# Gelu stage of a fused conv, expert and mixer block: bank rotation and fold of the partition groups

## The chip, the cores and the metric

One core of one Trainium2 chip runs the whole program in one launch. The metric is the device time in microseconds (us), from the program's first instruction to its last.

## The reference, cut to what matters

The program is a block of two convolution parts and two expert parts on 32 images of 256 channels and 14 x 14 points, which is 6272 tokens of 256 channels. The change lies in the last part: a mixture of 16 small experts for each of 8 heads, with two experts chosen for each token and head.

```python
h = x @ Wm + bm
t = h.reshape(bs * L_ * H, HD)                # H = 8 heads of HD = 32
w = jax.nn.softmax(t @ expert_emb, axis=-1)
topw, topi = jax.lax.top_k(w, K)              # 2 of 16
hmid = jax.nn.gelu(jnp.einsum('td,edi->tei', t, W1) + b1, approximate=False)   # 32 to 128
eo = jnp.einsum('tei,eio->teo', hmid, W2) + b2                                # 128 to 32
comb = (jnp.take_along_axis(eo, topi[:, :, None], axis=1) * topw[:, :, None]).sum(axis=1)
out = comb.reshape(bs, L_, d) @ Wo + bo
```

The kernel computes all 16 experts for each token and head, weighs each with its gate (zero where it isn't chosen), and adds them up.

## The kernel before, in words

**Tiles.** The Gelu stage is the last stage (from line 2125). A unit is 1024 columns: 4 heads of 256 tokens. There are 48 such units and a last one of 8 heads of 128 tokens (`UNITS`, `NU` = 49). Each unit has four groups of four experts (`NG` = 196 groups), and a group is worked on in blocks of 512 columns (`NB` = 2). `x_r` holds a unit's heads (two buffers), `hid` eight Gelu results, `wb` the gates of a group, spread over partitions (three buffers), `gacc` a unit's running sum (two buffers), `gsum` a group's weighed result (two buffers).

**Slots.** The work is written in slots k = 0 to 200, one group to a slot, and each engine walks the slots in order with semaphores between them. `gel` counts Gelus, `put` counts results in `psY`, `got` counts what DVE has taken from there, `acc` counts GpSimd's additions.

- PE in slot k runs `first(4k)` to `first(4k+3)` (L2258): the 32-to-128 products of one expert each, into a buffer of two banks, `psA[m % 3]`. Each waits until the Gelu three experts earlier has emptied that buffer. `second(k-1, b)` (L2269) makes the 128-to-32 products of the group before; the four experts go to four groups of 32 partitions of one bank, `psY[use % 2]`. In slots without extras block 0 stands after the third `first` and block 1 after the fourth, otherwise both after the third.
- ACT (L2321) runs one Gelu over 1024 columns for each `first`.
- DVE in slot k runs `weigh(k-1, b)` (L2331): it adds the bias, multiplies with the gates, and writes `gacc` (first group of a unit) or `gsum`. Then it runs one or two of the 16 steps of `route` (L1613), which make the gates of later tokens. Before `weigh` stand the extras of the slot: `finish`, `route_copy` and `combine`.
- GpSimd (L2247) adds `gsum` to `gacc` for groups 1, 2 and 3 of each unit. `weigh` of group 3 of a unit waits until GpSimd is done with group 1 (`acc` at least a - 1), since it reuses that `gsum` buffer.
- SP (L2226) in slot k issues `heads_load` (every fourth slot, four transfers), the loads and stores of `route`, `gates_load(k+2)` (four transfers of 128 KB, after `weigh` of group k-1), and the stores of the output.

**The fold.** After a unit's four groups `gacc` holds four partial sums, one in each group of 32 partitions. `fold(w)` (L2280), in slot 4w+6, multiplies with `foldm`, four stacked unit matrices, once for each head, so that a head's sum lands in its place in `psY`. `combine` (L2351) on DVE copies it to `comb`. `last` (L2291) multiplies a chunk of 256 tokens, two units, with Wo in two halves, and `finish` (L2358) adds bias and residual. `LAST`, `ROUTE` and `STEPS` (L2149 to L2165) hold the slots of these extras and are worked out by hand-written rules.

```python
wait(eng, Q["got"], done_group(g - 3))              # gates_load, SP
wait(eng, Q["gel"], m - 2)                          # first, PE
wait(eng, Q["acc"], a - 1)                          # weigh into gsum, DVE
wait(eng, Q["acc"], 3 * w + 3)                      # fold, PE
```

Of the kernel before, what the change touches and what calls it, by code (L numbers as in the profile page):

```python
# [81 lines left out]
def build(nc, x, c1T, c2T, c3T, invts, lut1, lut2, lut3, bn1, bn2, bn3, routerT, w_moe,  # L82
          se_w1T, se_b1, se_w2T, se_b2, se_wgT, se_bg, wm, bm, emb, w1, b1, w2, b2, wo, bo, out):
    with ExitStack() as ctx:
# [990 lines left out]
        Q = {k: sem(f"q_{k}") for k in ("w", "w2", "wo", "set", "hi", "mm1", "gel", "put", "got", "acc", "rt")}  # L1075
# [4 lines left out]
        q_st = [sem(f"q_st{a}") for a in range(2)]  # L1080
        w1_r = sb("w1_r", [128, NE, HID], F32R)
# [3 lines left out]
        foldm = sb("fold", [128, HD])  # L1085
# [523 lines left out]
        def gates_ps(use):  # L1609

            return ps4[:, 3, 64:64 + CH] if use < EARLY else psY[use % 2]
# [44 lines left out]
        def route_pe(eng, r, use):  # L1656

            wait(eng, Q["rt"], (r + 1) * RT2)
            wait(eng, Q["got"], use if r < EARLY else use - 1)
            for s in range(NSUB):  # L1660
                m = eng.transpose(gates_ps(use)[:, s * SUB:(s + 1) * SUB],  # L1661
                                  route_tile(r, M1)[:, s * NH:(s + 1) * NH].rearrange("p h e -> p (h e)"), ident[0:SUB, 0:SUB])
            m.then_inc(Q["put"], 1)

# [58 lines left out]
        with nc.Block() as block:  # L1723
# [34 lines left out]
            def _(eng):  # L1758
# [4 lines left out]
                eng.memset(foldm[:], 0.0).then_inc(Q["set"], 1)  # L1763
                for r in range(4):
                    eng.wait_ge(Q["set"], r + 3)

                    eng.affine_select(out=foldm[:], in_=foldm[:], compare_op=ALU.not_equal, fill=1.0,
                                      base=-32 * r, pattern=[[-1, HD]], channel_multiplier=1).then_inc(Q["set"], 1)
# [368 lines left out]
        comb = ex[:].rearrange("p h c -> p (h c)")[:, 0:2 * UT].rearrange("p (a c) -> p a c", a=2)  # L2137
# [4 lines left out]
        psA = [ctx.enter_context(nc.psum_tensor(f"psA{a}", [128, NB * BLK], F32)) for a in range(3)]  # L2142
        psY = [ctx.enter_context(nc.psum_tensor(f"psY{a}", [128, BLK], F32)) for a in range(2)]
# [5 lines left out]
        FOLD = {4 * w + 6: w for w in range(NU)}  # L2149
        LAST = {8 * c + 11 + m_: (c, m_) for c in range(len(PARTS) - 1) for m_ in range(2)}  # L2150
# [5 lines left out]
        for r in reversed(range(EARLY, T)):  # L2156
            over = min(over, NEEDED[r] - 6)
            while over + 2 in FOLD or over + 2 in LAST:
                over -= 1
# [3 lines left out]
            clear = [k for k in range(over, over + PACE) if k + 1 not in LAST]  # L2163
# [5 lines left out]
        EXTRAS, EXTRA_USE, BLOCK_USE, uses = {}, {}, {}, EARLY  # L2169
        for k in range(SLOTS):  # L2170
            EXTRAS[k] = [kind for kind, table in (("last", LAST), ("route", ROUTE), ("fold", FOLD)) if k in table]
            for kind in EXTRAS[k]:
                EXTRA_USE[kind, k] = uses
                uses += 1
            for b in range(NB if 0 < k <= NG else 0):
                BLOCK_USE[k - 1, b] = uses
                uses += 1

        def apart(k):

            return not EXTRAS[k] or (EXTRAS[k] == ["fold"] and k + 1 not in LAST)

# [35 lines left out]
        with nc.Block() as block:  # L2218
            @block.sync
            def _(eng):  # L2220
# [5 lines left out]
                for k in range(SLOTS):  # L2226
# [20 lines left out]
            def _(eng):  # L2247
                for w in range(NU):
                    for g in range(1, 4):
                        a = 3 * w + g - 1  # L2250

                        wait(eng, Q["got"], done_group(4 * w + g))
                        wait(eng, Q["acc"], a)
                        eng.tensor_tensor(gacc[:, w % 2], gacc[:, w % 2], gsum[:, a % 2], ALU.add).then_inc(Q["acc"], 1)  # L2254

            @block.tensor
            def _(eng):
                def first(m):  # L2258
# [4 lines left out]
                    wait(eng, Q["gel"], m - 2)  # L2263
                    for b in range(NB):
                        mm = eng.matmul(psA[m % 3][:, b * BLK:(b + 1) * BLK], w1_r[:, m % 16],  # L2265
# [3 lines left out]
                def second(g, b):  # L2269
# [10 lines left out]
                def fold(w, use):  # L2280
                    tok, n, head, heads = UNITS[w]

                    wait(eng, Q["acc"], 3 * w + 3)
                    wait(eng, Q["got"], use - 1)
                    for q in range(heads):
                        mm = eng.matmul(psY[use % 2][q % 4 * 32:q % 4 * 32 + 32, q // 4 * n:(q // 4 + 1) * n], foldm[:],  # L2286
                                        gacc[:, w % 2, q * n:(q + 1) * n], start=True, stop=True,
                                        tile_position=(0, q % 4 * 32))
                    mm.then_inc(Q["put"], 1)
# [10 lines left out]
                for k in range(SLOTS):  # L2300
# [4 lines left out]
                    for e in range(4):  # L2305
# [122 lines left out]
```

## Time and profile before

| | us |
|---|---|
| median of 3 runs (2325.78 to 2329.89) | 2328.03 |
| the profiled execution | 2325.96 |
| its span, first to last instruction | 2324.2 |
| busy in the span: PE, ACT, DVE, GpSimd (POOL) | 2050.6, 1286.3, 1336.8, 831.9 |
| all Gelus (784) | 809.7 |
| all products of `first`, all of `second` | 479.7, 399.9 |
| all products of the fold (400), all copies of `combine` (49) | 31.8, 20.8 |

The Gelu stage runs from about 1417 us to the end. Busy times of products overlap where they are pipelined, so a busy PE isn't PE at its peak; in the stage's own rows below each figure is from one profiled execution. Line numbers are the kernel's.

### The profile page before, as it was taken

To read this page: it belongs to the slowest core of one execution; us is meant where nothing else is said; L and a number is where in the kernel's file an instruction comes from. 1 tells how busy PE (TensorE), PEld (TensorE's weight loads), DVE (VectorE), ACT (ScalarE), POOL (GpSimd) and SP (SyncE) were. 2 spreads that over 40 slices of the span, in tenths; PEclk is the share of its full clock that TensorE was granted. 3 is DMA by queue.
4 is the path that set the end of the run, shared out by engine and by line. 5 is a ranking of instruction groups with operands and counts; after the bars stand their busy time and mean duration, and the time that the engine had idled before them with its cause. 6 is when DMAs were issued, how large, how long until landed. Compare 5 with 4: busy or idle time off the path is not lost. (4 is left out here: it accounts for less than half of the span.)

```text
span 2324.2 us, 36023 instructions
## 1 busy us (share of the span) xinstructions
PE 2050.6 (88%) x12850; PEld 1136.7 (49%) x12851; DVE 1336.8 (58%) x2117; ACT 1286.3 (55%) x1634; POOL 831.9 (36%) x608
## 2 busy tenths in 40 slices
PE   6999699999796783798499986999999999999998
PEld 3444355555454562677266553444444444444444
DVE  5666435554456874222388963666666666667533
ACT  3444312222354331122245425999989989999897
POOL 4333111211000777000688611444334443343443
PEclk8999869999798765999689988999999999999999
DMA  2110121220613442677324325666565666556654
GB/s 57 29 29 15 48 85 58 67 69 20 245 55 113 142 146 77 170 210 207 102 83 136 118 73 154 157 158 165 157 164 157 156 162 165 162 152 158 158 155 106
DMA packets 280563, 281.24 MB, mean 121 GB/s; under 512 B 44998, under 2 KB 261654, under 8 KB 280278
## 3 DMA queue, kind: packets, MB, share of 16 engines
q1 hardware_dynamic: 246422, 233.49, 36.6%
q0 software_dynamic: 12288, 25.72, 3.7%
q10 hardware_dynamic: 21696, 19.93, 2.5%
q8 instruction: 99, 1.62, 0.3%
q14 instruction: 58, 0.48, 0.1%
HBM read 203.76 MB, written 75.25 MB: 120 GB/s over the span
## 5 line engine op out<-in xcount | busy, mean ns | idle before, releaser
L2326 ACT ACTIVATE BIG<-psA,b_s 128x1024 f32<-128x1024 f32 x784 | 809.7, 1116 | 88.7 <-PE psA L2265 81.1
L2254 POOL TENSOR_TENSOR BIG<-BIG 128x1024 f32<-128x1024 f32 x147 | 359.4, 2445 | 552.1 <-DVE BIG L2347 552.1
L2265 PE MATMUL psA<-x_r,w_r 128*128 128x512 f32 x1568 | 479.7, 427 | 20.3 <-DMA x_r<-hs_d 12.1
L2347 DVE SCALAR_TENSOR_TENSOR BIG<-psY,b_s,BIG 128x512 f32<-128x512 f32 x392 | 291.6, 750 | 246.2 <-PE psY L2275 245.4
L2265 PEld LDWEIGHTS psA<-x_r,w_r 128*128 128x128 f32 x1568 | 268.7, 190 | 329.4 <-ACT BIG L2326 248.2
L2275 PE MATMUL psY<-BIG,w_s 128*32 128x512 f32 x3136 | 399.9, 600 | 3.6 <-DVE BIG L2347 2.9
L719 DVE TENSOR_REDUCE b_nm<-psN 112x32 f32<-112x512 f32 x128 | 83.1, 686 | 148.0 <-PE psN L616 147.6
L1199 POOL DMA_INDIRECT xg_d<-xnb,SLOT x128 | 135.1, 1056 | 80.8 <-DVE SLOT L1314 44.2
L1774 POOL DMA_INDIRECT gath<-yg_d,SLOT x128 | 140.1, 1095 | 38.5 <-issue 35.7
L2275 PEld LDWEIGHTS psY<-BIG,w_s 128*32 128x32 f32 x3136 | 73.5, 108 | 161.2 <-issue 90.5
L719 DVE TENSOR_REDUCE a_nm<-psN 98x32 f32<-98x512 f32 x128 | 82.4, 686 | 87.5 <-PE psN L607 87.3
L557 POOL CAST b_pat_r<-BIG 72x3584 fp32r<-72x3584 f32 x16 | 50.7, 3171 | 219.5 <-PE psN L616 212.6
L1535 PE MATMUL ps<-BIG,xv 128*128 x528 | 126.6, 383 | 2.2 <-ACT xv L1561 1.0
L1561 ACT ACTIVATE xv<-ps 128x512 f32<-128x512 f32 x66 | 39.4, 597 | 157.5 <-PE ps L1521 155.7
L775 ACT ACTIVATE b_exs<-ps 128x1568 f32<-128x1568 f32 x32 | 47.3, 1477 | 104.6 <-PE ps L585 104.6
L580 PE MATMUL ps<-BIG,b_wb 72*128 72x392 f32 x256 | 101.0, 541 | 4.0 <-DVE xv L725 4.0
L1535 PEld LDWEIGHTS ps<-BIG,xv 128*128 128x128 f32 x528 | 96.1, 192 | 14.2 <-issue 3.7
L1576 DVE COPY ex<-ps 128x512 f32<-128x512 f32 x33 | 22.8, 692 | 99.7 <-PE ps L1535 99.7
L616 PE MATMUL psN<-b_wb_r,b_pat_r 73*112 73x128 f32 x512 | 70.6, 285 | 9.3 <-POOL b_pat_r L557 8.5
L1521 PE MATMUL ps<-ident,xv 128*128 128x128 f32 x264 | 41.3, 281 | 41.1 <-DMA xv<-xg_d 25.3
L616 PEld LDWEIGHTS psN<-b_wb_r,b_pat_r 73*112 73x112 f32 x512 | 61.0, 193 | 30.3 <-DVE b_nm L719 13.4
L795 ACT ACTIVATE BIG<-psMO 128x196 f32<-128x196 f32 x32 | 10.7, 334 | 109.3 <-PE psMO L640 109.3
(394 smaller groups left out, 3192.8 us busy)
## 6 DMA issues: line engine op xcount, KB each, us to landing
BIG<-wt_d SPq DMA_DIRECT2D x784, 128.0 KB, 3.3
x_r<-hs_d SPq DMA_DIRECT2D x196, 128.0 KB, 3.6
xg_d<-ex SPq DMA_DIRECT2D x64, 264.0 KB, 3.7
xv<-xg_d SPq DMA_DIRECT2D x66, 256.0 KB, 3.2
BIG<-ypad_d SPq DMA_DIRECT2D x140, 120.0 KB
xv<-x SPq DMA_DIRECT2D x64, 196.0 KB, 2.7
hs_d<-xv SPq DMA_DIRECT2D x32, 392.0 KB, 3.3
yg_d<-ex ACTq DMA_DIRECT2D x33, 256.0 KB, 3.6
```

What stands on the lines that cost most here:

```text
L557: eng.tensor_copy(pat_r[0:KP].rearrange("p g (b r) -> p g b r", b=IMGS), pat[s % 3][:, :, :, 0:HH * PADW]).then_inc(S["vr"], 1)
L580: eng.matmul(ps4[:, i, 0:CH], w_, src, start=True, stop=False)
L616: mm = eng.matmul(psN[0:SR, bank, g * 128:(g + 1) * 128], pat_r[0:KR, bank * 4 + g, sub * SR:(sub + 1) * SR], wb_r[0:KR, bank * 4 + g], st ...
L719: eng.tensor_reduce(dst, src, AX.X, ALU.max, negate=True).then_inc(S["max"], 1)
L1199: eng.indirect_dma_start(xg_d.ap(), bass.IndirectOffsetOnAxis(ap=SLOT[:, t * NSUB + s, j:j + 1], axis=0), xnb[:, t % XB, s], None).then_in ...
L1535: m = eng.matmul(psZ[:, u, r * C:(r + 1) * C], xt[:, u, r, h * 128:(h + 1) * 128], w_moe_s[:, bass.ds(e * (2 * C) + h * C, C)], start=(h = ...
L1774: eng.indirect_dma_start(gath[:, c % GB, 2 * s + j], None, yg_d.ap(), bass.IndirectOffsetOnAxis(ap=SLOT[:, c * NSUB + s, j:j + 1], axis=0) ...
L2254: eng.tensor_tensor(gacc[:, w % 2], gacc[:, w % 2], gsum[:, a % 2], ALU.add).then_inc(Q["acc"], 1)
L2265: mm = eng.matmul(psA[m % 3][:, b * BLK:(b + 1) * BLK], w1_r[:, m % 16], x_r[:, w % 2, b * BLK:(b + 1) * BLK], start=True, stop=True)
L2275: mm = eng.matmul(psY[use % 2][32 * e:32 * e + 32, :], w2_s[:, g % 4 * 4 + e], hid[:, (4 * g + e) % 8, b * BLK:(b + 1) * BLK], start=True, ...
L2326: eng.activation(hid[:, m % 8], psA[m % 3][:], ACT.Gelu, bias=b1_s[:, m % 16:m % 16 + 1]).then_inc(Q["gel"], 1)
L2347: eng.scalar_tensor_tensor(out=dst, in0=psY[use % 2][:], scalar=b2_s[:, g % 4:g % 4 + 1], in1=wb[:, g % 3, b * BLK:(b + 1) * BLK], op0=ALU ...
```

## The change

Two parts of the program change, both in the Gelu stage.

- **Banks.** `psA` has four pairs of two banks (`PAIRS_PS`), `psY` is gone. A slot takes five pairs in turn: one for each `first` and one for both blocks of `second`, and each taker waits until the reader of four takes earlier is done. `last` and `route_pe` are guests in the pair that the previous slot's `second` used. Both blocks of `second` stand after the slot's four `first`. DVE runs the steps of `route` before the weighings of the slot and not after them.
- **Fold.** `fold`, `foldm` and `combine` are gone. `fold_move(w)` on SP, in slot 4w+5 behind `gates_load`, issues 16 transfers (32 in the last unit) that move each head's four partial sums, 32 partitions by 256 columns, to the head's partitions in `fold4`. `fold_add(w)` on GpSimd, ahead of the addition of group 1 of unit w+1, adds the four sums in two instructions, of 512 and of 256 columns, into `comb`, which has two buffers now. `last` waits for it. `LAST` moves to slots 8c+12 and 8c+14.

```diff
-        foldm = sb("fold", [128, HD])
...
-            wait(eng, Q["got"], use if r < EARLY else use - 1)
+            if r < EARLY:
+                wait(eng, Q["got"], use)
+            else:
+                wait_room(eng, use)
...
-                eng.memset(foldm[:], 0.0).then_inc(Q["set"], 1)
-                for r in range(4):
-                    eng.wait_ge(Q["set"], r + 3)
-                    eng.affine_select(out=foldm[:], in_=foldm[:], compare_op=ALU.not_equal, fill=1.0,
-                                      base=-32 * r, pattern=[[-1, HD]], channel_multiplier=1).then_inc(Q["set"], 1)
...
-        comb = ex[:].rearrange("p h c -> p (h c)")[:, 0:2 * UT].rearrange("p (a c) -> p a c", a=2)
+        spare = xv[:].rearrange("p a u h c -> p (a u h c)")
+        comb = spare[:, 0:4 * UT].rearrange("p (i a c) -> p i a c", i=2, a=2)
+        fold4 = spare[:, 4 * UT:12 * UT].rearrange("p (i e c) -> p i e c", i=2, e=4)
...
-        psA = [ctx.enter_context(nc.psum_tensor(f"psA{a}", [128, NB * BLK], F32)) for a in range(3)]
-        psY = [ctx.enter_context(nc.psum_tensor(f"psY{a}", [128, BLK], F32)) for a in range(2)]
+        PAIRS_PS = 4
+        psA = [ctx.enter_context(nc.psum_tensor(f"psA{a}", [128, NB * BLK], F32)) for a in range(PAIRS_PS)]
...
-        FOLD = {4 * w + 6: w for w in range(NU)}
-        LAST = {8 * c + 11 + m_: (c, m_) for c in range(len(PARTS) - 1) for m_ in range(2)}
+        FOLDED = {4 * w + 5: w for w in range(NU)}
+        LAST = {8 * c + 12 + 2 * m_: (c, m_) for c in range(len(PARTS) - 1) for m_ in range(2)}
...
-            while over + 2 in FOLD or over + 2 in LAST:
+            while over + 2 in LAST:
...
+        FIRST_PAIR, PAIR_OF, GUEST_OF, TAKEN = {}, {}, {}, []
+        def take(reader, count):
+            TAKEN.append((reader, count))
+            return len(TAKEN) - 1
         for k in range(SLOTS):
-            EXTRAS[k] = [kind for kind, table in (("last", LAST), ("route", ROUTE), ("fold", FOLD)) if k in table]
-            for kind in EXTRAS[k]:
-                EXTRA_USE[kind, k] = uses
-                uses += 1
-            for b in range(NB if 0 < k <= NG else 0):
-                BLOCK_USE[k - 1, b] = uses
-                uses += 1
-        def apart(k):
-            return not EXTRAS[k] or (EXTRAS[k] == ["fold"] and k + 1 not in LAST)
+            EXTRAS[k] = [kind for kind, table in (("last", LAST), ("route", ROUTE)) if k in table]
+            for e in range(4):
+                if k < NG:
+                    FIRST_PAIR[4 * k + e] = take("gel", 4 * k + e + 1)
+                for kind in EXTRAS[k] if e == 0 else ():
+                    EXTRA_USE[kind, k] = uses
+                    guest = k - 2 < NG
+                    PAIR_OF[uses] = PAIR_OF[BLOCK_USE[k - 2, 0]] if guest else take("got", uses + 1)
+                    if guest:
+                        GUEST_OF[uses] = BLOCK_USE[k - 2, 0]
+                        TAKEN[PAIR_OF[uses]] = ("got", uses + 1)
+                    uses += 1
+            if 0 < k <= NG:
+                pair = take("got", uses + NB)
+                for b in range(NB):
+                    BLOCK_USE[k - 1, b] = uses
+                    PAIR_OF[uses] = pair
+                    uses += 1
+        LAST_SLOT = {c: k for k, (c, m_) in LAST.items() if m_ == 1}
+        def bank_pair(use):
+            return psA[PAIR_OF[use] % PAIRS_PS]
+        def wait_pair(eng, pair):
+            if pair >= PAIRS_PS:
+                reader, count = TAKEN[pair - PAIRS_PS]
+                wait(eng, Q[reader], count)
+        def wait_room(eng, use):
+            if use in GUEST_OF:
+                wait(eng, Q["got"], GUEST_OF[use] + 1)
+            else:
+                wait_pair(eng, PAIR_OF[use])
...
+        def fold_move(eng, w):
+            tok, n, head, heads = UNITS[w]
+            wait(eng, Q["acc"], 3 * w + 3)
+            wait(eng, Q["comb"], w - 1)
+            for e in range(4):
+                for q in range(heads):
+                    eng.dma_start(fold4[q % 4 * 32:q % 4 * 32 + 32, w % 2, e, q // 4 * n:(q // 4 + 1) * n],
+                                  gacc[32 * e:32 * e + 32, w % 2, q * n:(q + 1) * n]).then_inc(q_fold[w % 2], 16)
...
+                    if k in FOLDED:
+                        fold_move(eng, FOLDED[k])
...
+                def fold_add(w):
+                    tok, n, head, heads = UNITS[w]
+                    f = fold4[:, w % 2]
+                    wait(eng, q_fold[w % 2], folded(w))
+                    eng.tensor_tensor(f[:, 0:2], f[:, 0:2], f[:, 2:4], ALU.add).then_inc(Q["half"], 1)
+                    wait(eng, Q["half"], w + 1)
+                    if w >= 4:
+                        wait(eng, Q["put"], EXTRA_USE["last", LAST_SLOT[w // 2 - 2]] + 1)
+                    if heads == NH:
+                        dst, parts = comb[:, w // 2 % 2, :, 0:n], [f[:, i].rearrange("p (a c) -> p a c", a=2) for i in range(2)]
+                    else:
+                        dst, parts = comb[:, w // 2 % 2, w % 2], [f[:, i] for i in range(2)]
+                    eng.tensor_tensor(dst, parts[0], parts[1], ALU.add).then_inc(Q["comb"], 1)
                 for w in range(NU):
                     for g in range(1, 4):
                         a = 3 * w + g - 1
+                        if g == 1 and w > 0:
+                            fold_add(w - 1)
...
+                fold_add(NU - 1)
...
-                    wait(eng, Q["gel"], m - 2)
+                    wait_pair(eng, FIRST_PAIR[m])
                     for b in range(NB):
-                        mm = eng.matmul(psA[m % 3][:, b * BLK:(b + 1) * BLK], w1_r[:, m % 16],
+                        mm = eng.matmul(psA[FIRST_PAIR[m] % PAIRS_PS][:, b * BLK:(b + 1) * BLK], w1_r[:, m % 16],
...
-                    wait(eng, Q["got"], use - 1)
+                    if b == 0:
+                        wait_room(eng, use)
                     for e in range(4):
-                        mm = eng.matmul(psY[use % 2][32 * e:32 * e + 32, :], w2_s[:, g % 4 * 4 + e],
+                        mm = eng.matmul(bank_pair(use)[32 * e:32 * e + 32, b * BLK:(b + 1) * BLK], w2_s[:, g % 4 * 4 + e],
...
-                    wait(eng, Q["got"], max(use - 1, EXTRA_USE["fold", 4 * min(2 * c + 1, NU - 1) + 6] + 1))
+                    wait(eng, Q["comb"], min(2 * c + 2, NU))
+                    wait_room(eng, use)
                     for h in range(2):
-                        mm = eng.matmul(psY[use % 2][:, 0:n], wo_s[:, h, m_ * 128:(m_ + 1) * 128], comb[:, h, 0:n],
+                        mm = eng.matmul(bank_pair(use)[:, 0:n], wo_s[:, h, m_ * 128:(m_ + 1) * 128], comb[:, c % 2, h, 0:n],
...
-                        if e == 2 and "fold" in EXTRAS[k]:
-                            fold(FOLD[k], EXTRA_USE["fold", k])
-                        for b in range(NB if 0 < k <= NG else 0):
-                            if e == (2 + b if apart(k) else 2):
-                                second(k - 1, b)
+                    for b in range(NB if 0 < k <= NG else 0):
+                        second(k - 1, b)
...
-                            wait(eng, Q["put"], EXTRA_USE["fold", 4 * w - 2] + 1)
+                            wait(eng, q_fold[w % 2], folded(w - 2))
...
-                    if "fold" in EXTRAS[k]:
-                        combine(FOLD[k], EXTRA_USE["fold", k])
+                    for r, i in STEPS.get(k, ()):
+                        route(eng, r, (i,))
                     for b in range(NB if 0 < k <= NG else 0):
                         weigh(k - 1, b)
-                    for r, i in STEPS.get(k, ()):
-                        route(eng, r, (i,))
...
```

## Rows read from the trace of the kernel before

**Rows 1.** Windows view: window, length; busy PE, PEld, DVE, ACT, POOL; PEclk, DMA, GB/s.
```profile
1541.84:1560.09 18.25, 17.98 (x111) 8.08 (x109) 10.51 (x14) 16.77 (x17) 6.90 (x3) 1.00 0.61 157
```
**Rows 2.** Waits view from 1400 us on: waiter <- whom: us in total, times, longest.
```profile
ACT BIG L2326 <- PE psA L2265: 81.1, 132, 4.2
```
**Rows 3.** Timeline: start us, duration, engine, line; the fold of units 0 and 47.
```profile
1447.82 0.64 PE L2286 MATMUL psY<-BIG,fold 128*32 128x256 f32 x8
...
2303.90 0.64 PE L2286 MATMUL psY<-BIG,fold 128*32 128x256 f32 x8
```
**Rows 4.** Timeline of ACT: four Gelus in a row.
```profile
1509.45 4.13 ACT L2326 ACTIVATE BIG<-psA,b_s 128x1024 f32<-128x1024 f32 x4 [0.65 <-PE psA L2265]
```
**Rows 5.** Timeline of SP's queue: issues of stores, heads and gates.
```profile
1511.42 0.90 SPq L2241 DMA_DIRECT2D out<-BIG  x2
1512.37 1.97 SPq L2205 DMA_DIRECT2D x_r<-hs_d  x4
1514.44 1.80 SPq L2215 DMA_DIRECT2D BIG<-wt_d  x4
1516.28 0.90 SPq L2241 DMA_DIRECT2D out<-BIG  x2
```
**Rows 6.** Timeline of SP's queue: four loads of 32 partitions each, and the next issue.
```profile
1116.01 1.81 SPq L1734 DMA_DIRECT2D BIG<-w  x4
1117.86 0.42 SPq L1735 DMA_DIRECT2D b_s<-b  x1
```
**Rows 7.** DMA view: issues, KB of each, median us from issue to landing.
```profile
BIG<-wt_d SPq DMA_DIRECT2D x784, 128.0 KB, 3.3
...
out<-BIG SPq DMA_DIRECT2D x2, 34.0 KB, 1.6
...
out<-BIG SPq DMA_DIRECT2D x2, 30.0 KB, 4.1
```
**Rows 8.** Groups by line, GpSimd: busy us, mean ns of one, idle before.
```profile
L2254 POOL TENSOR_TENSOR BIG<-BIG 128x1024 f32<-128x1024 f32 x147 | 359.4, 2445 | 552.1 <-DVE BIG L2347 552.1
...
L540 POOL TENSOR_TENSOR a_xh<-xv 128x392 f32<-128x392 f32 x16 | 16.5, 1031 | 0.0
```
**Rows 9.** Timeline of the tail: last accumulation, last fold, first product of `last`.
```profile
2315.73 2.34 POOL L2254 TENSOR_TENSOR BIG<-BIG 128x1024 f32<-128x1024 f32 x1 [1.43 <-DVE BIG L2347]
2318.12 0.63 PEld L2286 LDWEIGHTS psY<-BIG,fold 128*32 128x32 f32 x16 [4.20 <-POOL BIG L2254]
...
2319.74 2.07 PE L2296 MATMUL psY<-ex,wo_s 128*128 128x128 f32 x8 [0.55 <-DVE ex L2356]
```
**Rows 10.** Timeline in mid-stage: `second` and its weighings; `first`, the `second` behind it, `first`.
```profile
1506.83 1.92 PE L2275 MATMUL psY<-BIG,w_s 128*32 128x512 f32 x16
...
1508.06 1.51 DVE L2347 SCALAR_TENSOR_TENSOR BIG<-psY,b_s,BIG 128x512 f32<-128x512 f32 x2 [1.57 <-PE psY L2275]
...
1517.07 0.73 PE L2265 MATMUL psA<-x_r,w_r 128*128 128x512 f32 x2
...
1517.73 1.07 PE L2275 MATMUL psY<-BIG,w_s 128*32 128x512 f32 x8
...
1518.73 1.67 PE L2265 MATMUL psA<-x_r,w_r 128*128 128x512 f32 x6
```
**Rows 11.** Windows view (columns of rows 1): PE idle, and the stretches after a restart.
```profile
802.00:806.70 4.70, 0.01 (x1) 0.00 (x0) 4.36 (x12) 0.99 (x3) 3.48 (x5) 0.79 0.38 124
806.70:810.00 3.30, 3.27 (x30) 3.17 (x30) 3.13 (x11) 1.41 (x2) 2.69 (x3) 0.50 0.23 66
...
1417.40:1422.50 5.10, 5.08 (x12) 3.44 (x12) 0.00 (x0) 3.82 (x4) 0.00 (x0) 0.50 0.89 221
1422.60:1427.80 5.20, 5.20 (x28) 1.96 (x26) 0.00 (x0) 5.01 (x6) 0.00 (x0) 1.00 1.13 215
```
**Rows 12.** Groups by line, DVE from 1400 us on: two steps of `route`.
```profile
L1636 DVE TENSOR_TENSOR rt<-rt,rs 98x512 f32<-98x512 f32 x28 | 53.2, 1900 | 0.7
...
L1632 DVE TENSOR_TENSOR rt<-rt,rev 98x512 f32<-98x512 f32 x28 | 19.3, 688 | 0.7
```

More of the change, by code:

```diff
@@ L1072, in build @@
         yg_d = nc.dram_tensor("yg_d", [TILES * ROWS, C], F32)
-        Q = {k: sem(f"q_{k}") for k in ("w", "w2", "wo", "set", "hi", "mm1", "gel", "put", "got", "acc", "rt")}
+        Q = {k: sem(f"q_{k}") for k in ("w", "w2", "wo", "set", "hi", "mm1", "gel", "put", "got", "acc", "half", "comb", "rt")}
         q_wst = sem("q_wst")
@@ L1080, in build @@
         q_st = [sem(f"q_st{a}") for a in range(2)]
+        q_fold = [sem(f"q_fold{a}") for a in range(2)]
         w1_r = sb("w1_r", [128, NE, HID], F32R)
@@ L1609, in gates_ps @@
         def gates_ps(use):
-            return ps4[:, 3, 64:64 + CH] if use < EARLY else psY[use % 2]
+            return ps4[:, 3, 64:64 + CH] if use < EARLY else bank_pair(use)
         def route(eng, r, steps):
@@ L2162, in build @@
             LOADS.setdefault(max(0, over - 2), []).append(r)
-            clear = [k for k in range(over, over + PACE) if k + 1 not in LAST]
+            clear = list(range(over, over + PACE))
             for i in range(RT2):
@@ L2198, in tokens, with folded @@
             return V[:].rearrange("p h t c -> p h (t c)")[:, :, tok:tok + n]
+        def folded(w):
+            return 16 * sum(4 * UNITS[u][3] for u in range(w % 2, w + 1, 2))
+        def fold_move(eng, w):
[6 more added lines that the diff above has]
+                                  gacc[32 * e:32 * e + 32, w % 2, q * n:(q + 1) * n]).then_inc(q_fold[w % 2], 16)
         def heads_load(eng, w):
@@ L2278, in second @@
                     mm.then_inc(Q["put"], 1)
[L2280 to L2289, printed above, removed]
                 def last(c, m_, use):
                     n = PARTS[c][1]
-                    wait(eng, Q["got"], max(use - 1, EXTRA_USE["fold", 4 * min(2 * c + 1, NU - 1) + 6] + 1))
+                    wait(eng, Q["comb"], min(2 * c + 2, NU))
+                    wait_room(eng, use)
                     for h in range(2):
-                        mm = eng.matmul(psY[use % 2][:, 0:n], wo_s[:, h, m_ * 128:(m_ + 1) * 128], comb[:, h, 0:n],
+                        mm = eng.matmul(bank_pair(use)[:, 0:n], wo_s[:, h, m_ * 128:(m_ + 1) * 128], comb[:, c % 2, h, 0:n],
                                         start=(h == 0), stop=(h == 1))
@@ L2325, in _ @@
                     wait(eng, Q["mm1"], m + 1)
-                    eng.activation(hid[:, m % 8], psA[m % 3][:], ACT.Gelu,
+                    eng.activation(hid[:, m % 8], psA[FIRST_PAIR[m] % PAIRS_PS][:], ACT.Gelu,
                                    bias=b1_s[:, m % 16:m % 16 + 1]).then_inc(Q["gel"], 1)
@@ L2346, in weigh @@
                     wait(eng, Q["put"], use + 1)
-                    eng.scalar_tensor_tensor(out=dst, in0=psY[use % 2][:], scalar=b2_s[:, g % 4:g % 4 + 1],
+                    eng.scalar_tensor_tensor(out=dst, in0=bank_pair(use)[:, b * BLK:(b + 1) * BLK], scalar=b2_s[:, g % 4:g % 4 + 1],
                                              in1=wb[:, g % 3, b * BLK:(b + 1) * BLK], op0=ALU.add,
                                              op1=ALU.mult).then_inc(Q["got"], 1)
-                def combine(w, use):
-                    tok, n, head, heads = UNITS[w]
-                    wait(eng, Q["put"], use + 1)
-                    dst = comb[:, 0:2, 0:n] if heads == NH else comb[:, w % 2, 0:n]
-                    src = psY[use % 2][:, 0:2 * n].rearrange("p (a c) -> p a c", a=2) if heads == NH else psY[use % 2][:, 0:n]
-                    eng.tensor_copy(dst, src).then_inc(Q["got"], 1)
                 def finish(c, m_, use):
@@ L2362, in finish @@
                     wait(eng, q_st[m_], stored(c))
-                    eng.scalar_tensor_tensor(out=fin[:, m_, 0:n], in0=psY[use % 2][:, 0:n], scalar=bo_s[:, m_:m_ + 1],
+                    eng.scalar_tensor_tensor(out=fin[:, m_, 0:n], in0=bank_pair(use)[:, 0:n], scalar=bo_s[:, m_:m_ + 1],
                                              in1=tokens(c)[:, m_], op0=ALU.add, op1=ALU.add).then_inc(Q["got"], 1)
```

## The prediction

> **What bounds the kernel now.** The windows view comes first. In a stretch of 18.25 us of the Gelu stage, the time of one unit (four slots), PE is busy for 17.98 us and ACT for 16.77 us at full clock [rows 1]: two engines near their limit, PE the nearer. The waits view then says that ACT still waits 81.1 us in all, 132 times, for `first`'s products [rows 2]: PE, in its fixed order, comes late now and then. The period is read from two starts of the fold, 47 units apart: (2303.90 - 1447.82) / 47 = 18.2 us a unit [rows 3]. Four Gelus take 4.13 us [rows 4], so ACT alone would need 16.5 us. What a better rotation can win is at most the difference, 1.7 us in each of 49 units, 83 us.
>
> **What is removed or moved.** The fold's products and DVE's copy leave PE and DVE, both banks of `psY` join the rotation, and a slot's two `second` calls stand together at its end. I cost all this at zero beyond the floor of 16.5 us: Two products of `first` take 0.73 us, six 1.67, so 0.235 for each further one, and the sixteen of `second` 1.92 [rows 10]: a slot of 4.13 us then holds some 8 x 0.235 + 1.92 = 3.8 us of products, and the next slots absorb what a `last` adds. If that cover were gone, the floor would be today's 18.2. DVE runs `route` before, not after, the two weighings of a slot; between one slot's weighings and the next the same steps run as now. The constants of `foldm` sit in a stage that waits for other things.
>
> **What is added, and where it lies.** In each unit SP issues 16 transfers (32 in the last one) at slot 4w+5, behind `gates_load` and ahead of everything later on SP. Such an instruction costs SP time: two stores start 0.95 us before the next instruction, 0.475 us each [rows 5]. The new transfers have 32 partitions, and the four loads of 32 partitions earlier in the trace took (1117.86 - 1116.01) / 4 = 0.46 us each [rows 6]. I take 0.475. SP's load in a unit becomes 16 + 4 + 16 issues for gates, heads and fold and about 3.3 for stores and gates' tables, 39.3 x 0.475 = 18.7 us, already above ACT's 16.5.
>
> The worse cost is a chain of waits. GpSimd runs `fold_add(w-1)` ahead of `acc` for group 4w+1, its queue's next entry. `weigh` of group 4w+3 reuses a `gsum` buffer, so it waits for that addition. `first(4(4w+5)+3)` on PE needs the bank pair which that weighing reads. Behind it stand the products of group 4w+4, and the weighing of group 4w+4 releases the next `gates_load` and with it the next sixteen transfers. So a loop closes once a unit. With zero at the end of the weighing of group 4w:
> - SP's gates group: 0.1 + 1.84 (1514.44 to 1516.28) [rows 5] = 1.94
> - fifteen issues until the last transfer starts, 15 x 0.475: 9.07
> - that transfer lands. No move inside SBUF stands in the trace. The bounds are the stores of 34 KB, 1.6 us, and of 30 KB, 4.1 us, with 3.3 us for the 128 KB loads [rows 7]. I take 2.2, nearer the lower end, since nothing else is queued then: 11.27
> - GpSimd: 1024 elements take 2.445 us and 392 take 1.03 us [rows 8], that is 2.24 ns an element. So 512 take 1.3, 256 take 0.75, then the delayed accumulation 2.45, and three handovers of 0.05 (2315.73 + 2.34 to 2318.12 [rows 9]): 15.9
> - two weighings, 0.05 + 1.51 [rows 10]: 17.5
> - `first` to `second` on PE, 0.05 + 0.66 (1517.07 to 1517.73), then from the first product to the end of both weighings 2.74 (1506.83 to 1508.06 + 1.51) [rows 10]: 20.9 us.
>
> That already exceeds 18.7 and 16.5, so the loop decides, and SP is not even the limit. The later gates are covered: those of group 4w+4 are issued by 11.4 and land by 14.7 [rows 7], and their weighing starts at 19.4.
>
> The Trainium skill puts a price on landing: the page "DMA: Bandwidth & Descriptors", section "Anatomy of one DMA", fits about 2.0 us plus bytes over 436 GB/s for the software path. An estimate by that page is 2.1 us here, which would make the sum 5 us lower. No run so far shows such a move.
>
> One more term: PE has 4 x 3.8 = 15.2 us of products in such a unit of 20.9, and of the 5.7 that are left I put 4 to 5 us in front of that `first`, where it waits longest. In this trace an idle stretch of 4.7 us ended with the clock granted at 0.50, 1.2 GHz [rows 11]. After another restart PE was busy without a break for 5.1 us at 0.50 before it was granted 1.00, 2.4 GHz [rows 11]. PE's part of the loop's last step, 0.66 + 1.9 us, would thus run mostly at half rate: +2.2 us, and 0 if the clock holds. I take 2.2: **23.1 us a unit**. It lies between 20.3 (clock held, landing 1.6) and 25.0 (landing 4.1).
>
> **DVE beside GpSimd.** L1636 takes 1.90 us on average where the like L1632 takes 0.69 [rows 12]: it meets the accumulation. The two new additions, 2.05 us a unit, can hold a `route` step as long. In most units DVE waits in `weigh` at that moment, so I take nothing; up to 1 us a unit goes to the upper end.
>
> **Sum.** The loop runs between the weighings of groups 4 and 192, 47 times: 47 x (23.1 - 18.2) = +230 us. The unit before it runs at ACT's rate, -1.7. From group 192 to 195 it takes 17.5 us, not three slots of 4.55: +3.8. In the tail the last accumulation ends 0.8 later, and 31 x 0.475 + 2.2 + 2.3 = 19.2 us of transfers and additions replace 1.6 us of product and copy (2318.12 to 2319.74 [rows 9]): +17.6, +18.4 in all. The ends together: +20. The profiled execution took 2325.96 us, of which 2324.2 is its span, and that is 2.1 us below the median of the runs. 2326 + 230 + 20 = **2576 us**; against the median it would be some 2 us more.
>
> **The rivals.**
> 1. The same loop, clock held: 20.9 us a unit, 2326 + 47 x 2.7 + 20 = 2473 us. For it: an idle time that splits into shorter pieces, since the slots before the stall have waits of their own. Against it: the 4.7 us that ended at 0.50 [rows 11]. Chance 0.25.
> 2. Only SP's load binds, because the rotation absorbs the late weighing: 18.7 us a unit, 2326 + 47 x 0.5 + 20 = 2370 us. For it: four pairs hold more in flight than today's buffers. Against it: `first` and `weigh` wait on exactly these buffers, as worked out above. Chance 0.07.
> 3. Faster: issuing a move inside SBUF costs SP little. Its place is the term 15 x 0.475. At 0.05 us an issue the loop takes 14.5 us, ACT's 16.5 decides, and the ends come to +1: 2326 - 47 x 1.7 + 1 = 2247 us. It decides below (18.2 - 13.8) / 15 = 0.29 us an issue. Against it: every transfer in this stage, whatever its size, holds SP for 0.43 us or more when issues follow each other closely [rows 5, 6]. Chance 0.08. The Trainium skill, page "DMA: Bandwidth & Descriptors", section "Issuing engines are not separate DMA queues", says that the time the sequencer takes to initiate a transfer is usually small beside the transfer. By that rule this rival would come true. The rows speak against it here: 0.475 us, sixteen times, against a landing of a few microseconds that is paid once.
>
> **How the numbers follow.** The forecast has 0.60, the rivals 0.25, 0.07 and 0.08. The range takes in the forecast and rival 1 with their bounds: below, clock held and landing 1.6, 2473 - 28 = 2445; above, landing 4.1, 2576 + 89 = 2665. That gives 2445 to 2665. About 0.2% is what a measurement of this kernel can tell from no change. Slower by more is every case but rival 3, and I leave 0.01 for a balance of issue cost and floor: faster 0.08, same 0.01, slower 0.91.
>
> **What would show it.** If right: the starts of the fold's transfers lie 21 to 24 us apart. Once a unit GpSimd waits for DMA before the short additions, DVE waits for GpSimd before the weighing of group 4w+3, and PE's longest waits are for DVE. ACT's share of the stage falls to 16.5 / 23.1, or 0.7, and PEclk shows digits below 9. SP's sixteen moves take 7 to 8 us, and the tail after the last weighing some 28 us. Wrong: SP issues that take under 0.3 us, Gelus without gaps, a clock that holds at 1.00, or a weighing of group 4w+3 that no longer waits for GpSimd.

## The result and the profile after

The changed kernel takes 2716.8 us (median of 4 runs, 2713.8 to 2718.8) against 2326.9 for the kernel before: 1.168 times the time, 95% interval 1.165 to 1.171. The profiled execution took 2716.5 us, its span is 2714.3.

All of it lies in the Gelu stage. The ends of the weighings of groups 4 and 192 stand at 1436.3 and 2662.1 us in the timeline of after, at 1447.1 and 2303.2 in that of before: (2662.1 - 1436.3) / 47 = 26.1 us a unit, where [rows 3] gave 18.2. Units take turns: those whose loop meets no slot of `last` on PE take 25.2 us on average, those that meet one 27.0.

The waits view of the changed kernel from 1400 us on (waiter <- whom: us in total, times, longest) answers to [rows 2]:

```profile
POOL xv L2300 <- DMA xv<-BIG: 753.4, 49, 21.7
ACT BIG L2380 <- PE psA L2331: 453.8, 118, 10.9
...
PE psA L2353 <- POOL xv L2309: 215.3, 25, 26.0
DVE BIG L2401 <- POOL BIG L2319: 207.9, 24, 10.2
...
PE psA L2331 <- DVE BIG L2401: 146.5, 24, 6.8
```

GpSimd waits for the transfers once a unit, 15 us each time. DVE waits for GpSimd's accumulation and PE's `first` for DVE, but 24 times each, in half of the units. ACT waits for PE, 453.8 us in place of 81.1. One line is new to the prediction: `last` (L2353) waits for GpSimd's second addition, 215 us in 25 times.

Here is one unit without `last` in the loop, in the timeline (start, duration, engine, line), from the weighings of its first group to those of the next unit's:

```profile
1902.70 1.51 DVE L2401 SCALAR_TENSOR_TENSOR BIG<-psA,b_s,BIG 128x512 f32<-128x512 f32 x2 [1.10 <-PE psA L2342]
...
1904.28 2.52 SPq L2261 DMA_DIRECT2D BIG<-wt_d  x4
...
1906.90 10.03 SPq L2243 DMA_DIRECT2D xv<-BIG  x16
...
1917.03 1.95 SPq L2261 DMA_DIRECT2D BIG<-wt_d  x4
...
1918.29 1.26 POOL L2300 TENSOR_TENSOR xv<-xv 128x512 f32<-128x512 f32 x1 [15.17 <-DMA xv<-BIG]
...
1919.64 0.72 POOL L2309 TENSOR_TENSOR xv<-xv 128x256 f32<-128x256 f32 x1
...
1920.32 7.60 POOL L2319 TENSOR_TENSOR BIG<-BIG 128x1024 f32<-128x1024 f32 x3
...
1922.74 1.41 DVE L2401 SCALAR_TENSOR_TENSOR BIG<-psA,b_s,BIG 128x512 f32<-128x512 f32 x2 [9.22 <-POOL BIG L2319]
1924.07 1.62 DVE L1629 TENSOR_TENSOR rt<-rt,rs 98x512 f32<-98x512 f32 x1
...
1924.21 1.22 PE L2331 MATMUL psA<-x_r,w_r 128*128 128x512 f32 x2 [6.33 <-DVE BIG L2401]
...
1925.36 3.12 PE L2342 MATMUL psA<-BIG,w_s 128*32 128x512 f32 x16
...
1928.39 1.40 DVE L2401 SCALAR_TENSOR_TENSOR BIG<-psA,b_s,BIG 128x512 f32<-128x512 f32 x2
```

In this kind of unit it is the predicted loop, link by link. In the unit behind it the loop runs another way:

```profile
1931.71 10.58 SPq L2243 DMA_DIRECT2D xv<-BIG  x16
...
1943.60 1.26 POOL L2300 TENSOR_TENSOR xv<-xv 128x512 f32<-128x512 f32 x1 [15.69 <-DMA xv<-BIG]
1944.94 0.72 POOL L2309 TENSOR_TENSOR xv<-xv 128x256 f32<-128x256 f32 x1
...
1945.72 2.07 PE L2353 MATMUL psA<-xv,wo_s 128*128 128x256 f32 x4 [8.58 <-POOL xv L2309]
...
1952.21 1.51 DVE L2401 SCALAR_TENSOR_TENSOR BIG<-psA,b_s,BIG 128x512 f32<-128x512 f32 x2 [1.18 <-PE psA L2342]
...
1956.14 1.51 DVE L2401 SCALAR_TENSOR_TENSOR BIG<-psA,b_s,BIG 128x512 f32<-128x512 f32 x2 [1.81 <-PE psA L2342]
```

PE stands at `last`, one slot ahead of the predicted stall, until GpSimd's second addition is done. The delayed weighing at 1952.21 then waits for PE's products and no longer for GpSimd's accumulation.

In the first of the two units sixteen moves keep SP busy from 1906.90 to 1917.03, (1917.03 - 1906.90) / 16 = 0.633 us each; the two stores of [rows 5] take 0.475 each. The transfers themselves land fast, as the DMA view says (KB of each, median us from issue to landing):

```profile
BIG<-wt_d SPq DMA_DIRECT2D x784, 128.0 KB, 3.3
...
xv<-BIG SPq DMA_DIRECT2D x768, 32.0 KB, 1.9
```

The windows view of the first unit (window, length; busy PE, PEld, DVE, ACT, POOL; PEclk, DMA, GB/s) answers to [rows 11]: PE is idle for 6.3 us and restarts at 0.50.

```profile
1904.20:1917.90 13.70, 13.68 (x80) 6.49 (x78) 5.63 (x10) 13.24 (x14) 0.00 (x0) 1.00 0.30 83
1917.90:1924.20 6.30, 0.00 (x0) 0.00 (x0) 1.46 (x3) 2.20 (x3) 5.68 (x4) 0.75 0.69 184
1924.20:1927.40 3.20, 3.19 (x14) 1.10 (x18) 3.17 (x2) 1.11 (x1) 3.06 (x2) 0.50 1.06 240
```

The tail answers to [rows 9]: 32 moves at 0.64 us stand between the last accumulation and the last products.

```profile
2683.65 2.34 POOL L2319 TENSOR_TENSOR BIG<-BIG 128x1024 f32<-128x1024 f32 x1 [1.37 <-DVE BIG L2401]
...
2686.02 20.36 SPq L2243 DMA_DIRECT2D xv<-BIG  x32
...
2709.76 2.07 PE L2353 MATMUL psA<-xv,wo_s 128*128 128x128 f32 x8 [25.96 <-POOL xv L2309]
```

SP still waited for DVE after all, so its load alone isn't the limit (waits view of SP's queue, from 1424 us on):

```profile
SPq L48 <- DVE BIG L2401: 211.2, 85, 5.5
```

### The profile page after: what moved, and what is told of

Read it like the earlier page. It is cut to its first block and busy times, and to the rows that moved or that the text cites. A ratio compares the mean times of both kernels' runs of the same rounds, so it can differ in the third digit from the quotient of the medians.

```text
span 2714.3 us, 35959 instructions
## 1 busy us (share of the span) xinstructions
PE 2094.9 (77%) x12450; PEld 1181.5 (44%) x12451; DVE 1307.9 (48%) x2068; ACT 1282.2 (47%) x1634; POOL 923.6 (34%) x701
## 5 line engine op out<-in xcount | busy, mean ns | idle before, releaser
L2380 ACT ACTIVATE BIG<-psA,b_s 128x1024 f32<-128x1024 f32 x784 | 805.4, 1128 | 457.0 <-PE psA L2331 453.8
L2331 PE MATMUL psA<-x_r,w_r 128*128 128x512 f32 x1568 | 491.8, 449 | 158.8 <-DVE BIG L2401 146.5
L2401 DVE SCALAR_TENSOR_TENSOR BIG<-psA,b_s,BIG 128x512 f32<-128x512 f32 x392 | 290.5, 749 | 500.9 <-PE psA L2342 291.3
L2331 PEld LDWEIGHTS psA<-x_r,w_r 128*128 128x128 f32 x1568 | 297.1, 205 | 414.7 <-DVE BIG L2401 158.1
L2342 PE MATMUL psA<-BIG,w_s 128*32 128x512 f32 x3136 | 418.0, 654 | 0.5 <-ACT BIG L2380 0.3
L2300 POOL TENSOR_TENSOR xv<-xv 128x512 f32<-128x512 f32 x49 | 61.9, 1262 | 753.4 <-DMA xv<-BIG 753.4
L2353 PE MATMUL psA<-xv,wo_s 128*128 128x256 f32 (+1 forms) x200 | 76.6, 523 | 215.3 <-POOL xv L2309 215.3
L2342 PEld LDWEIGHTS psA<-BIG,w_s 128*32 128x32 f32 x3136 | 92.4, 116 | 217.7 <-issue 149.5
L2410 DVE SCALAR_TENSOR_TENSOR BIG<-psA,bo_s,V 128x256 f32<-128x256 f32 (+1 forms) x50 | 23.9, 478 | 280.5 <-PE psA L2353 280.5
L2353 PEld LDWEIGHTS psA<-xv,wo_s 128*128 128x128 f32 x200 | 48.0, 259 | 235.5 <-POOL xv L2309 226.7
```

Source lines behind the costliest of these rows:

```text
L2300: eng.tensor_tensor(f[:, 0:2], f[:, 0:2], f[:, 2:4], ALU.add).then_inc(Q["half"], 1)
L2331: mm = eng.matmul(psA[FIRST_PAIR[m] % PAIRS_PS][:, b * BLK:(b + 1) * BLK], w1_r[:, m % 16], x_r[:, w % 2, b * BLK:(b + 1) * BLK], start=Tr ...
L2342: mm = eng.matmul(bank_pair(use)[32 * e:32 * e + 32, b * BLK:(b + 1) * BLK], w2_s[:, g % 4 * 4 + e], hid[:, (4 * g + e) % 8, b * BLK:(b + ...
L2353: mm = eng.matmul(bank_pair(use)[:, 0:n], wo_s[:, h, m_ * 128:(m_ + 1) * 128], comb[:, c % 2, h, 0:n], start=(h == 0), stop=(h == 1))
L2380: eng.activation(hid[:, m % 8], psA[FIRST_PAIR[m] % PAIRS_PS][:], ACT.Gelu, bias=b1_s[:, m % 16:m % 16 + 1]).then_inc(Q["gel"], 1)
L2401: eng.scalar_tensor_tensor(out=dst, in0=bank_pair(use)[:, b * BLK:(b + 1) * BLK], scalar=b2_s[:, g % 4:g % 4 + 1], in1=wb[:, g % 3, b * BL ...
```

## The experiments

Three theories stood against each other: the **loop** of waits, the **queue** (SP's load alone sets 26.1 us a unit), and the **banks** (the new rotation is slow). Times a unit below are read as above, from the ends of the weighings of groups 4 and 192. The two kernels named rotation_products were executed six times each, the others once.

**late_add** takes the transfers out of the loop: GpSimd makes the fold's additions behind the unit's accumulations, and `last` comes later, so that it finds the sums.

```diff
-                        if g == 1 and w > 0:
-                            fold_add(w - 1)
                         ...
                         eng.tensor_tensor(gacc[:, w % 2], gacc[:, w % 2], gsum[:, a % 2], ALU.add).then_inc(Q["acc"], 1)
+                    if w > 0:
+                        fold_add(w - 1)
...
-        LAST = {8 * c + 12 + 2 * m_: (c, m_) for c in range(len(PARTS) - 1) for m_ in range(2)}
-        LAST.update({4 * NU + 3 + m_: (len(PARTS) - 1, m_) for m_ in range(2)})
+        LAST = {8 * c + 14 + m_: (c, m_) for c in range(len(PARTS) - 1) for m_ in range(2)}
+        LAST.update({4 * NU + 4 + m_: (len(PARTS) - 1, m_) for m_ in range(2)})
...
-        SLOTS = 4 * NU + 5
+        SLOTS = 4 * NU + 6
```

> GpSimd adds the moved parts of a unit behind all three accumulations of the next unit instead of ahead of the first, and the products of a chunk with Wo come two slots later, so that they find the sums. Loop theory (the chain issue, landing, addition, delayed accumulation, delayed weighing, delayed products sets 26.1 us a unit): the chain is cut, and the next limit is SP's own load, 23.3 issues of 0.475 us and 16 of 0.63 in a unit, 21.2 us. 2716 - 47 x 4.9 = about 2486 us. Queue theory (SP's load already sets the 26.1 us): no change, 2716 within 15. Bank theory (the new rotation itself is slow): no change.

Measured: 2530.8 us, (2485.5 - 1436.3) / 47 = 22.3 us a unit. The loop was the limit: 186 us are gone, of which late_last below puts 39 down to the slots of `last` and leaves 147 for the additions. What is left is the queue: SP's waits for DVE have shrunk from 211 to 12 us, and SP's load of issues sets the pace. It is 1.1 us a unit more than estimated, for which no run gives the reason. The waits view of SP's queue, from 1430 us on:

```profile
SPq L48 <- DVE BIG L2400: 11.6, 8, 2.9
```

**half_moves** moves two of the four partial sums.

```diff
-            return 16 * sum(4 * UNITS[u][3] for u in range(w % 2, w + 1, 2))
+            return 16 * sum(2 * UNITS[u][3] for u in range(w % 2, w + 1, 2))
-            for e in range(4):
+            for e in range(2):
```

> Only the first two of a head's four partial sums are moved, 8 transfers a unit and 16 in the last one; the other two parts that GpSimd adds are old contents, so half of the fold is left out. Loop and queue theory alike: 8 issues of 0.63 us fewer in each of 47 units and 16 fewer in the tail, 2716 - 237 - 10 = about 2470 us, with the later additions still waiting for the transfers. Bank theory: at most the tail changes, about 2705 us.

Measured: 2432.0 us, (2394.1 - 1444.6) / 47 = 20.2 us a unit, 5.9 less. That is the eight issues, 8 x 0.633 = 5.1 us, and 0.8 more, whose cause stays open; the whole lies 38 us below the expected 2470. The time follows the number of issues. Nothing was changed in the banks' rotation, so at least these 285 us aren't the banks'.

**from_hbm** has the same sixteen transfers, read from HBM.

```diff
-                                  gacc[32 * e:32 * e + 32, w % 2, q * n:(q + 1) * n]).then_inc(q_fold[w % 2], 16)
+                                  wt_d.ap()[tok // UT].rearrange("h e n -> (h e) n")[32 * e:32 * e + 32, 0:n]).then_inc(q_fold[w % 2], 16)
```

> The same number of transfers with the same places to go, 32 rows of 1 KB each, but read from the gates' table in HBM and not from the running sum in SBUF: the sum of the four partition groups is left out. If the 0.63 us an issue comes from the source in SBUF, an issue falls to 0.47 as for the loads, the loop is shorter by 15 x 0.16 = 2.4 us and the landing longer by 0 to 1.4: 23.7 to 25.1 us a unit, 2603 to 2670 us. If the price comes from the shape of 32 rows or from issuing sixteen in a row, nothing changes: 2716 us.

Measured: 2596.6 us, (2550.4 - 1442.8) / 47 = 23.6 us a unit, just below the expected stretch. In SP's timeline sixteen moves now take (1926.78 - 1919.34) / 16 = 0.465 us each, and they land in 1.8 us, no later than those from SBUF. So the shape of 32 rows isn't what costs; a source in SBUF for a destination in SBUF is. The 120 us saved are about what the forecast's 0.475 left out. The timeline of SP's queue (start, duration, engine, line), and a line of the DMA view:

```profile
1919.34 7.34 SPq L2243 DMA_DIRECT2D xv<-wt_d  x16
1926.78 1.80 SPq L2261 DMA_DIRECT2D BIG<-wt_d  x4
```
```profile
xv<-wt_d SPq DMA_DIRECT2D x768, 32.0 KB, 1.8
```

**old_banks_moves** undoes the rotation, with the order of the second products and of DVE's steps, and keeps the fold by transfers.

```diff
-        PAIRS_PS = 4
-        psA = [ctx.enter_context(nc.psum_tensor(f"psA{a}", [128, NB * BLK], F32)) for a in range(PAIRS_PS)]
+        psA = [ctx.enter_context(nc.psum_tensor(f"psA{a}", [128, NB * BLK], F32)) for a in range(3)]
+        psY = [ctx.enter_context(nc.psum_tensor(f"psY{a}", [128, BLK], F32)) for a in range(2)]
...
-                    wait_pair(eng, FIRST_PAIR[m])
+                    wait(eng, Q["gel"], m - 2)
```

> The banks and the order of the kernel before (three buffers of two banks, two single banks, blocks of the second products apart), with the fold by transfers and additions. Loop theory: the chain runs over the single banks just as well, 24 to 27 us a unit, 2620 to 2760 us. Bank theory: the rotation is the cause, and this is back near the kernel before, 2326 and some 20 us of tail.

Measured: 2725.6 us, (2671.2 - 1441.0) / 47 = 26.2 us a unit. The bank theory falls: the time a unit is the same over `psY` as over the pairs.

**late_last** moves only the slots of `last`, by the lines on `LAST` and `SLOTS` in the diff of late_add.

> Only the slots of the products with Wo move, from 8c+12 and 8c+14 to 8c+14 and 8c+15, and the last chunk's by one. If their new wait for GpSimd's sums costs time of its own (PE stands 215 us before them, 25 times), the units with such a slot fall from 26.9 to the 25.2 us of the others: 23 to 24 x 1.7 = 40 us less, about 2676 us. If that wait only stands where another one would, nothing changes: 2716 us.

Measured: 2677.7 us, 39 less than the changed kernel; (2624.9 - 1443.8) / 47 = 25.1 us a unit. The wait of `last` costs time of its own: in every other unit it stood at slot 8c+12 on PE, ahead of three `first` and the products of group 4w+3. These units fall from 27.0 to 24.9 us on average; the others, 25.2 before, take 25.3.

**late_last_busy** is late_last, with PE's idle time filled with repeated products.

```diff
-                    for b in range(NB):
+                    for b in [b for _ in range(12 if m % 16 == 6 and w > 0 else 1) for b in range(NB)]:
                         mm = eng.matmul(psA[FIRST_PAIR[m] % PAIRS_PS][:, b * BLK:(b + 1) * BLK], w1_r[:, m % 16],
```

> As the run before, and PE makes one pair of products of each unit, the one ahead of the stall, twelve times over into the same bank with the same result, some 4.7 us more of work where it would stand idle. If the fallen clock after the stall costs what the traces show (5.64 us from the delayed weighing to the next one against 3.45 at full clock), the granted clock stays at 1.00 there and a unit is 1.5 to 2.2 us shorter: 70 to 105 us below the run before. If the clock costs nothing in the loop, the time is that of the run before or up to 30 us longer.

Measured: 2662.2 us, 15.5 below the run before, less than expected, and hardly more than single executions differ by (eleven of the kernel before, taken with no_moves, lie between 2318.8 and 2332.0 us). The mean granted clock did rise, as the windows view shows; the first line is late_last, the second this run:

```profile
1424.00:2640.00 1216.00, 931.70 (x4932) 420.09 (x4930) 493.42 (x674) 804.57 (x780) 441.18 (x240) 0.86 0.52 136
```
```profile
1424.00:2640.00 1216.00, 1096.50 (x5976) 601.64 (x5974) 495.14 (x677) 806.71 (x777) 454.21 (x243) 0.97 0.53 135
```

With the clock up, the loop's last step is back at full speed: from the end of the delayed weighings, 1640.95, to that of the next, 1644.41, it is 3.46 us. The timeline of this run, columns as above:

```profile
1639.54 1.41 DVE L2401 SCALAR_TENSOR_TENSOR BIG<-psA,b_s,BIG 128x512 f32<-128x512 f32 x2 [8.53 <-POOL BIG L2319]
...
1641.00 0.74 PE L2331 MATMUL psA<-x_r,w_r 128*128 128x512 f32 x2 [1.26 <-DVE BIG L2401]
...
1642.90 1.51 DVE L2401 SCALAR_TENSOR_TENSOR BIG<-psA,b_s,BIG 128x512 f32<-128x512 f32 x2
```

Half of the units run at 23.8 us or less (median of late_last: 25.2). But 7 of the 47 take 29.7 to 31.6 us. There `route_pe` stands between, waits for the bank that the delayed weighing reads, and the twelve pairs come behind the stall and not in it, as another stretch of the same timeline shows:

```profile
1663.04 0.89 PE L1664 MATMUL psA<-ident,rt 98*128 98x98 f32 x4 [5.29 <-DVE BIG L2401]
...
1663.63 7.85 PE L2331 MATMUL psA<-x_r,w_r 128*128 128x512 f32 x28
```

In seven more units, each right behind one of those, the granted clock is up, 1.00 from 1690.00 to 1697.00 in the one shown, and the loop's last step still takes 5.7 us, there from 1693.40 to 1699.06. Two `route` steps of DVE run beside GpSimd's accumulations and hold the weighing up:

```profile
1689.50 7.69 POOL L2319 TENSOR_TENSOR BIG<-BIG 128x1024 f32<-128x1024 f32 x3
1691.99 1.41 DVE L2401 SCALAR_TENSOR_TENSOR BIG<-psA,b_s,BIG 128x512 f32<-128x512 f32 x2 [9.27 <-POOL BIG L2319]
...
1693.32 1.64 DVE L1629 TENSOR_TENSOR rt<-rt,rs 98x512 f32<-98x512 f32 x1
...
1695.00 2.74 DVE L1632 TENSOR_TENSOR rt<-rt,rev 98x512 f32<-98x512 f32 x1
...
1697.66 1.40 DVE L2401 SCALAR_TENSOR_TENSOR BIG<-psA,b_s,BIG 128x512 f32<-128x512 f32 x2
```

So the clock's part in the loop is shown, some 2 us in the units where the filling lay in the stall. The 40 units outside the seven long ones take 23.7 us on average, 1.4 less than late_last's 25.1. Over 47 units that would be 66 us, an estimate from these two runs; the long units gave most of it back.

**no_moves** leaves the transfers out, with `last` as in late_last.

```diff
-                    if k in FOLDED:
-                        fold_move(eng, FOLDED[k])
...
-                    wait(eng, q_fold[w % 2], folded(w))
...
-                            wait(eng, q_fold[w % 2], folded(w - 2))
+                            wait(eng, Q["acc"], 3 * (w - 2) + 3)
```

> The rotation with GpSimd's additions and the later products with Wo, but no transfers at all: GpSimd adds what lies in the buffer, so the fold's sums are left out. Loop theory: without issue and landing the chain is gone, the additions of 2 us a unit hide in GpSimd's idle time, and ACT and PE set 16.6 to 17.6 us a unit, the tail loses 22 us: 2677 - 47 x (25.1 - 17.1) - 22 = about 2280 us, between 2255 and 2303. If the additions, or the wait of the first addition behind them, cost time of their own, it stays above 2330.

Measured: 2259.6 us, (2238.8 - 1439.9) / 47 = 17.0 us a unit. GpSimd's additions hide. Transfers, their issue and the waits behind them cost 2677.7 - 2259.6 = 418 us, more than the 351 by which late_last is slower than the kernel before: without them the rotation, additions included, is 67 us faster than that kernel.

**rotation_products** is the rotation with the new order on DVE and without the fold by transfers: the fold is a product again, a guest as `last` is, DVE copies it, and `LAST` has the slots of the kernel before.

```diff
-                    if k in FOLDED:
-                        fold_move(eng, FOLDED[k])
...
+                        if e == 0 and "fold" in EXTRAS[k]:
+                            fold(FOLD[k], EXTRA_USE["fold", k])
...
+                    if "fold" in EXTRAS[k]:
+                        combine(FOLD[k], EXTRA_USE["fold", k])
                     for r, i in STEPS.get(k, ()):
```

> The bank rotation, the new order of the second products and of DVE, with the fold by products and DVE's copy as before, as guests in the rotation. If the fold by transfers is the whole loss, what is left is the rotation's own worth: between ACT's 16.5 us a unit and the 18.2 of the kernel before, 47 x 0 to 47 x 1.7 and up to 10 us at the start of the stage less than 2327, so 2237 to 2327, about 2260 us. Bank theory: above 2400 us.

Measured: 2295.3 us, 0.987 of the kernel before (0.985 to 0.990), (2274.4 - 1449.9) / 47 = 17.5 us a unit. It beats both kernels and is the version to keep. ACT's wait for PE has fallen from 81.1 us in [rows 2] to 54.1 (waits view, from 1400 us on):

```profile
ACT BIG L2361 <- PE psA L2299: 54.1, 151, 4.4
```

**rotation_products_steps_after** puts DVE's `route` steps behind the weighings again.

```diff
-                    for r, i in STEPS.get(k, ()):
-                        route(eng, r, (i,))
                     for b in range(NB if 0 < k <= NG else 0):
                         weigh(k - 1, b)
+                    for r, i in STEPS.get(k, ()):
+                        route(eng, r, (i,))
```

> The rotation with the fold by products, and DVE's route steps behind the weighings of a slot as in the kernel before. If the order of DVE carries a part of the gain of that version (the guests' banks are read ahead of the route steps), it is 5 to 25 us slower than 2295; if all of it comes from the banks, the two agree within 5 us.

Measured: 2343.3 us, 1.008 of the kernel before (1.007 to 1.010), 48 us more than with the steps ahead, where 5 to 25 were expected. A guest's bank is read late when the steps of the slot before stand ahead of `finish` or `route_copy`, and the fourth `first` waits for it, as the waits view says (from 1400 us on). The two lines of PE below are missing in the version with the steps ahead; they hold 24.5 us, while ACT's wait for PE is up by 46:

```profile
ACT BIG L2361 <- PE psA L2299: 100.4, 168, 4.3
...
PE psA L2299 <- DVE BIG L2398: 15.3, 7, 2.2
...
PE psA L2299 <- DVE wts L1672: 9.2, 13, 0.7
```

One more edit of the change bears on this, and the list of the change doesn't name it. The kernel before kept `route` steps out of the slot ahead of a `last`; all versions here but old_banks_moves have lost that rule, this one too:

```diff
-            clear = [k for k in range(over, over + PACE) if k + 1 not in LAST]
+            clear = list(range(over, over + PACE))
```

So with the old order on DVE and without the rule the rotation loses. Whether it would lose with the rule put back was not tried.

## Why the prediction was wrong in size, and how far its mechanism held

The direction and the loop hold, and in every other unit all of its links; the range of 2445 to 2665 us doesn't hold the 2717. Step by step, for the first unit shown above:

- SP's gates group: 1.94 forecast, 1904.28 to 1906.90 and 0.07 before it measured, 2.7; other groups of that trace take 1.8 to 2.0.
- **Fifteen issues, 7.13 forecast, 15 x 0.633 = 9.5 measured.** This is the term that failed, "I take 0.475", from loads out of HBM and stores into it, and it stood without an upper bound although no move inside SBUF was in the trace. from_hbm gives its worth: 120 us. With issues of 0.465, and `last` where it stood, it took 2596.6 us, inside the range. One line of the argument for 0.475 was read too widely: [rows 6] lie ahead of this stage, and the last of them is 0.42, not "0.43 us or more".
- Landing 2.2 forecast, 1.9 measured. GpSimd 4.65 forecast, 1918.29 to 1922.74 (the weighing's start) = 4.45 measured. Two weighings 1.56 forecast, 1.4 measured.
- PE's step with the fallen clock: 3.45 + 2.2 = 5.65 forecast, 1924.15 to 1929.79 = 5.64 measured; 3.46 with the clock up. In the units with `last` the stall lies one slot earlier, the granted clock is 1.00 again by this step (1953.70 to 1957.65), and it takes 1953.72 to 1957.65 = 3.93.
- **A wait that was not named.** The prediction followed GpSimd's queue to `acc` and `weigh`, but not the other reader of the sums: `last` waits for `fold_add` in PE's queue. late_last gives its worth: 39 us. In these units the path runs over `last` and not over the delayed accumulation.
- The "4 to 5 us" of idle PE in front of that `first` were 6.3 in that unit, as the issues took longer.
- The tail was forecast with 31 x 0.475; the moves took 20.4 us.

With both errors put right, 2576 + 120 + 39, and 47 x 0.3 = 14 less for the landing, the sum is 2721, where 2717 was measured. That it comes so near is luck in part, for the ends were forecast at +20 and came to +20 by two errors. The time behind group 192 grew from 21.0 to 52.2 us, by 31.2 and not by 3.8 + 18.4 = 22.2. The weighing of group 4 ended 10.8 us earlier and not 1.7, and 6.5 of these lie ahead of the stage, whose first product starts at 1417.42 us before and at 1410.92 after.

The range also left out the microsecond a unit that the prediction put "to the upper end" for DVE; with it the bound would have been 2665 + 47 = 2712, still too low.

The rivals: the clock did not hold, so the first is out. The second, SP's load alone, is the next limit behind the loop, at 22.3 and not 18.7 us a unit, as late_add shows. The third asked for an issue below 0.29 us; it is 0.633 here. Sixteen issues take 10.1 us, one landing 1.9. The Trainium skill, page "DMA: Bandwidth & Descriptors", section "Issuing engines are not separate DMA queues", calls the time to initiate a transfer usually small beside the transfer; by these numbers that does not hold for sixteen short ones in a row.

That "in most units DVE waits in `weigh`", so that the `route` steps beside GpSimd cost nothing, held for the changed kernel: in 17 of the 24 units without `last` that weighing waits for PE. In the other seven, the one shown among them, DVE's steps end last, at about 1928.4, but it takes 5.6 to 5.7 us to the end of both weighings there and 4.9 to 5.7 in the others, for at half clock the second product block comes late as well. late_last_busy shows what the clock hid: with the clock up the same two steps cost 5.66 - 3.46 = 2.2 us.

What the rotation's other edits are worth, costed at zero against a floor of 16.5 us, is 17.0 us a unit in no_moves and 17.5 with the fold by products. That the move of the `route` steps changes nothing was wrong at least for the rotation with the fold by products, where it decides over 48 us; in the changed kernel itself it was not tried.

## What to carry to other kernels

Price a transfer by its issue on the queue, with the ends that it has (here SBUF to SBUF), times the count; sixteen short ones behind each other are a serial stage of 10 us, however fast each lands. When work moves to a waiting queue, list every reader of its result and every instruction behind the wait, and look for the way back to its own start: a wait that closes a loop costs its whole length once a turn. And change one part at a time: the rotation with the new order on DVE gains 1.3%, and the fold by transfers hid it. When one term of a loop is taken away, look for the one that it hid: in late_last_busy two steps on DVE took the place of the clock.

## What the runs showed of the hardware that was not expected

A transfer from SBUF to SBUF holds SP for 0.633 us from one issue to the next (after, 1906.90 to 1917.03), one of the same 32 rows of 1 KB from HBM for 0.465 (from_hbm, 1919.34 to 1926.78), in the same place of the program. Landing is equal, 1.9 and 1.8 us.

PE's clock fell in the stall of the first shown unit: 6.3 us idle, then 0.50 (1.2 GHz) over the next 3.2 us of full work. Repeating products in the idle time kept the mean granted clock of the stage at 0.97 in place of 0.86.

Two `route` steps of DVE took 1.64 and 2.74 us beside GpSimd's accumulations (late_last_busy, from 1693.32), where [rows 12] have 0.69 for the second on average.
